# A fused Mamba and quantised-FFN kernel: copies out of PSUM one or two slots later in ScalarE's order, and z's first quarter in the other PSUM bank

## The chip, the core and the metric

The kernel runs on 1 core of one Trainium2 chip. The metric is the device time of one execution in microseconds (us); less is better. Engines go by the profile's names: PE is TensorE's matmuls and PEld its weight loads, DVE is VectorE, ACT is ScalarE, POOL is GpSimd, SP is SyncE.

## What is computed

Two inputs of 2 x 2048 tokens are folded into one stream, and one layer adds two branches to it. Cut to what matters here:

```python
# branch 1: a small conditioning scan, then a Mamba block (D_INNER 1024, D_STATE 16)
xn = layernorm(cond_scan(x))                       # 64 states, projection back to 512
x_br, z = split(xn @ W_in)                         # 1024 and 1024
xb = silu(causal_conv4(x_br) + conv_b)
Bm, Cm = xb @ W_b, xb @ W_c                        # 16 and 16
delta = softplus(xb @ W_delta + b_delta)           # 1024
h = exp(delta * A) * h + delta * Bm * xb           # per channel and state, over 2048 steps
y = sum(h * Cm) + xb * Dp
x = x + (y * silu(z)) @ W_out + residual
# branch 2: low-rank modulated layer, then a bit-linear FFN 512 -> 2048 -> 512 with GELU
x = x + ffn(cond2(x, cond))
```

## The kernel before

The file has two phases. `scan_phase` does branch 1, `ffn_phase` branch 2; the change is in `scan_phase` alone.

**Blocks and slots.** The 4096 tokens are cut into 16 blocks of 256 (`NBLK`, `T`). Every engine runs the same list of steps (`run_steps`): step -1 prepares block 0, step k scans block k while it prepares block k+1 and finishes block k-1, step 16 finishes the last block. A step has 32 slots (`NQ`), one for each of 8 channel tiles of 128 (`dt`) times 4 groups (`g`) of 4 states. All orders are written out by hand, slot by slot; engines meet only at semaphores, and each engine takes its own list strictly in order.

**What one slot q is.** ACT computes four `exp(delta * A)` into one of two PSUM buffers `a_ps` (L688, with `wait(act, s_scan, NQ * k + q - 1)`: the scan of slot q-2 has to be done). DVE multiplies u by B into one of four ring buffers (L842, helper `bx`), one slot ahead, and runs the scan (L850, helper `scans`). POOL saves the last column (L462) and multiplies the ring buffer by C in two halves (L469). PE sums the states by transposing each half into `yT_ps` (L1053, helper `turn_states`), and only then is the ring buffer free: `bx(q)` waits until `turn_states(q-4)` is done (`wait(dve, s_tr, NQ * k + q + 1 - RING)`). In slots 3 mod 4 `bx` first refreshes a column of B (L833, L839), and in slots 7, 15, 23 also computes u from delta and xb (L821); in slots 1 mod 4 DVE gates a finished tile with z (L785).

**The work beside the scan.** The other matmuls go to two PSUM banks, `work[0]` and `work[1]`. The table `BANK` names the bank of every job and, by its order, the turn: PE's `give(job)` waits until the job before it in the same bank has been copied out, and ACT's `take(job)` waits until PE has filled it. The jobs of block k+1 in the order of step k are: PRJ, WO0, WO1, YT, YB (conditioning scan and layer norm), XB0 to XB3 (x and the convolution, L992, copied by `xcopy`, L562), a Silu over x (`silu`, L571, with two ACT table loads around it), Z0 to Z3 (the quarters of z, L1000, copied by `zcopy`, L555; silu of z in `zsilu`, L579), BC (B and C, L1008, which needs the finished Silu, copied by `bc`, L585), and DL0 to DL3 (delta, L1019; `dexp`, `dtail`, `dln` are L597/L599, L606, L610, with a table load at L610 and one back at L688). Between them stand WOUT0 and WOUT1 (output rows of block k-1, L1035, copied by `wout`, L513) and GT0 to GT3 (gated tiles, L1063, copied by `gT`, L620). PE's slots are in the dictionary `plan`, ACT's in `next_plan`, `scan_plan`, `turned` and `back_plan`. y0 goes back through `y0back` (L533, L535), and x(0, 0) waits for it.

**Delta's second part** is one addition of 128x1024 elements on POOL (`delta_sum`, L420). `SUMS = (27, 6)` gives its slots: in 27 for the first half of the next block, in 6 for the second half of this block; in POOL's list it stands ahead of that slot's L462 and L469.

```python
def give(job):
    wait(pe, free[BANK[job]], jobs_before(job, k))
    return work[BANK[job]]
def take(job, step_of=k):
    act.wait_ge(full[BANK[job]], jobs_before(job, step_of) + 1)
    return work[BANK[job]]
```

Of the kernel before, what the change touches and what calls it, by code (L numbers as in the profile page):

```python
# [19 lines left out]
ND = DI // P  # L20
# [21 lines left out]
NV = 228  # L42


SUMS = (27, 6)
BANK = {"PRJ": 0, "GT3": 1, "WOUT0": 1, "WO0": 0, "WO1": 0, "WOUT1": 1, "YT": 0, "YB": 0, "GT0": 1,
        "XB0": 0, "XB1": 1, "XB2": 0, "XB3": 1, "Z0": 0, "BC": 0, "GT1": 1, "Z1": 1, "DL0": 0,
        "DL1": 1, "Z2": 0, "Z3": 0, "GT2": 1, "DL2": 0, "DL3": 1}
BACK = ["GT3", "WOUT0", "WOUT1"]
TURN = ["GT0", "GT1", "GT2"]  # L50
# [18 lines left out]
def wait(eng, sem, value):  # L69

    if isinstance(value, int) and value <= 0:
        return
    eng.wait_ge(sem, value)


def scan_phase(nc, V, big, s_big, vec, xT_in, w_p, w_s, w_o, w_in, w_bc, w_delta, w_out, f_w1, f_w2, c2_w1, c2_w2,
# [3 lines left out]
    with ctx:  # L80
# [271 lines left out]
        def _(pool):  # L352
# [61 lines left out]
            def delta_sum(pair, b, bp):  # L414

                for j in (2 * pair, 2 * pair + 1):
                    pool.wait_ge(free[BANK[f"DL{j}"]], jobs_before(f"DL{j}", b - 1) + 1)
                pool.wait_ge(s_dln, 2 * b + pair + 1)
                d = delta[:, bp, 4 * pair:4 * pair + 4, :].rearrange("p a b -> p (a b)")
                nc.gpsimd.tensor_tensor(d, d, ln_full[:, :], ALU.add).then_inc(s_delta, 1)  # L420

            def step(k, par, front, back, scan):
                for q in range(NQ):
                    dt, g = q // NG, q % NG
                    if scan and q == SUMS[1]:
                        delta_sum(1, k, par)
                    if front and q == SUMS[0]:
                        delta_sum(0, k + 1, 1 - par)
# [46 lines left out]
        def _(act):  # L475
# [8 lines left out]
            def step(k, par, front, back, scan):  # L484
                n, fp = k + 1, 1 - par
# [19 lines left out]
                def wout(tt):  # L505
                    job = f"WOUT{tt}"
                    ps = take(job)

                    if tt:
                        act.wait_ge(s_st[0], 16 * k)  # L510
                    else:
                        act.wait_ge(s_st[1], 16 * k)
                    nc.scalar.activation(x2row[:, :], ps[:, :], ACT.Copy).then_inc(free[BANK[job]], 1)  # L513

                def stats(tt):
                    job = f"WO{tt}"
# [33 lines left out]
                def zcopy(j):  # L550
                    ps = take(f"Z{j}")
                    if j == 0:

                        wait(act, s_gate, ND * k)
                    nc.scalar.activation(zs[:, fp, j // 2, 512 * (j % 2):512 * (j % 2) + 512], ps[:, :], ACT.Copy)\  # L555
                        .then_inc(free[BANK[f"Z{j}"]], 1)

                def xcopy(j):
                    ps = take(f"XB{j}")
                    for m in range(2):  # L560
                        mt = 2 * j + m
                        r = nc.scalar.activation(xb[:, fp, mt, :], ps[:, T * m:T * m + T], ACT.Identity,  # L562
                                                 bias=V[:, V_CB + mt:V_CB + mt + 1])
                    r.then_inc(free[BANK[f"XB{j}"]], 1)
# [22 lines left out]
                def dexp(j, late):  # L587

                    ps = take(f"DL{j}", k - 1 if late else k)
                    b = k if late else n  # L590
                    if j >= 2:

                        act.wait_ge(s_delta, 2 * b + 1)
                    for m in range(2):
                        mt = 2 * j + m
                        bias = V[:, V_BD + mt:V_BD + mt + 1]
                        nc.scalar.activation(lnbuf[:, j % 2, T * m:T * m + T], ps[:, T * m:T * m + T], ACT.Abs,  # L597
                                             bias=bias).then_inc(s_dexp, 1)
                        r = nc.scalar.activation(delta[:, par if late else fp, mt, :], ps[:, T * m:T * m + T],  # L599
                                                 ACT.Relu, bias=bias)  # L600
                    r.then_inc(free[BANK[f"DL{j}"]], 1)

                def dtail(pair, late):
                    b = k if late else n
                    act.wait_ge(s_dexp, 8 * b + 4 * pair + 4)
                    nc.scalar.activation(ln_full[:, :], ln_full[:, :], ACT.Exp, scale=-1.0).then_inc(s_dmin, 1)  # L606

                def dln(pair, late):
                    act.wait_ge(s_dmin, 2 * (k if late else n) + pair + 1)
                    nc.scalar.activation(ln_full[:, :], ln_full[:, :], ACT.Ln, bias=1.0).then_inc(s_dln, 1)  # L610
# [6 lines left out]
                def gT(pair, gp):  # L617

                    ps = take(f"GT{pair}")
                    nc.scalar.activation(xb[:, gp, 2 * pair:2 * pair + 2, :],  # L620
                                         ps[:, :].rearrange("p (m t) -> p m t", m=2), ACT.Copy)\
                        .then_inc(free[BANK[f"GT{pair}"]], 1)
# [8 lines left out]
                def rowcopy(c):  # L631
# [4 lines left out]
                    else:  # L636
# [2 lines left out]


                next_plan = {5: [prj], 6: [prj_ln], 8: [lambda: stats(0)], 9: [lambda: stats(1)], 10: [y0scale],
                             11: [y0back], 13: [lambda: xcopy(0)], 14: [lambda: xcopy(1)], 16: [lambda: xcopy(2)],
                             17: [lambda: xcopy(3), silu], 18: [lambda: zcopy(0)], 19: [bc], 21: [lambda: zcopy(1)],
                             23: [lambda: dexp(0, False)], 26: [lambda: zcopy(2)],
                             27: [lambda: dexp(1, False), lambda: dtail(0, False), lambda: zcopy(3)],
                             28: [lambda: dln(0, False)], 30: [zsilu], 31: [lambda: dexp(2, False)]}
                scan_plan = {2: [lambda: dexp(3, True), lambda: dtail(1, True)], 6: [lambda: dln(1, True)]}
                turned = {13: 0, 20: 1, 28: 2}
                back_plan = {6: [lambda: gT(ND // 2 - 1, fp)], 9: [lambda: wout(0)], 11: [lambda: wout(1)]}
                for q in range(NQ + 1):  # L650
                    dt, g = q // NG, q % NG
                    if scan and q == FIRST[1] + 3:
# [33 lines left out]
                    for i in range(G):  # L686
                        s = G * g + i
# [199 lines left out]
        def _(pe):  # L887
# [13 lines left out]
            def step(k, par, front, back, scan):  # L901
                n, fp = k + 1, 1 - par
# [121 lines left out]
                def wout(tt, part):  # L1024
                    job = f"WOUT{tt}"
                    ps = work[BANK[job]]
                    if part == 0:
                        give(job)

                        pe.wait_ge(free[BANK["GT3"]], jobs_before("GT3", k) + 1)  # L1030
                        pe.wait_ge(s_c0, 6 * k)
                        kept = y0[:, :] if isinstance(k, int) and k == NBLK else y0k[:, fp, :]
                        pe.matmul(ps[:, :], kept[:, P * tt:P * tt + P], Wo[:, :], start=True, stop=False)
                    for d in ((0, 1), (2, 3, 4), (5, 6, 7))[part]:
                        r = pe.matmul(ps[:, :], xb[:, fp, d, P * tt:P * tt + P], Wout[:, d, :],  # L1035
                                      start=False, stop=(d == ND - 1))
                    if part == 2:
                        r.then_inc(full[BANK[job]], 1)
# [48 lines left out]
                def factor_row(c):  # L1087
# [6 lines left out]
                    for d in range(KD):  # L1094
# [9 lines left out]
                        9: [("n", turn_back), ("b", wout, 1, 2)], 10: [("n", x, 0, 0)],  # L1104
                        11: [("s", turn_gated, 0, k), ("n", x, 0, 1)], 12: [("n", x, 1, 0), ("n", x, 1, 1)],
                        13: [("n", x, 2, 0)], 14: [("n", x, 2, 1), ("n", x, 3, 0)], 15: [("n", x, 3, 1)],
                        16: [("n", z, 0)], 17: [("n", bc)], 18: [("s", turn_gated, 1, k)],
                        19: [("n", z, 1), ("n", dl, 0, 0)], 20: [("n", dl, 0, 1)],
                        21: [("n", dl, 0, 2), ("n", dl, 0, 3)], 22: [("n", dl, 1, 0)],
                        23: [("n", dl, 1, 1), ("n", dl, 1, 2)], 24: [("n", dl, 1, 3), ("n", z, 2)], 25: [("n", z, 3)],  # L1110
                        26: [("s", turn_gated, 2, k), ("n", dl, 2, 0)], 27: [("n", dl, 2, 1)],
                        28: [("n", dl, 2, 2), ("n", dl, 2, 3)], 29: [("n", dl, 3, 0)],
                        30: [("n", dl, 3, 1), ("n", dl, 3, 2)], 31: [("n", dl, 3, 3)]}
                if isinstance(k, int) and k == 0:

# [542 lines left out]
```

## Time and profile before

| what | value |
|---|---|
| time, median of 3 runs | 2754.73 us (2754.4 to 2756.45) |
| the profiled execution: its time, its span | 2753.85 us, 2751.0 us |
| first scan starts (end of step -1) | 117.34 us |
| scans of blocks 0 to 14, start to start of the next block | 1963.03 us together |
| block 15 and step 16, then the FFN | the rest of the span |
| busy: PE, DVE, ACT, POOL | 2349.6, 2281.2, 1717.7, 1727.1 us |
| granted TensorE clock, mean | 0.937 |

The span is what the hardware profiler covers, and the time is 2.85 us more. Times in rows are microseconds from the span's start. A row of the timeline may hold several like instructions in a run (xN), with the time from the first start to the last end. The bracket is idle time of that engine before the row and what ended it; a semaphore wait of several conditions is put down to the one that came last. An fp32 matmul counts twice in xN, a transpose once.

### The profile page before, as it was taken

Reading aid. Unit: us, or ns where it says so; the run is one execution under the profiler, and the core shown is the slowest. Engines: PE = TensorE matmul, PEld = TensorE weight load, DVE = VectorE, ACT = ScalarE, POOL = GpSimd, SP = SyncE. Lnnn points to the kernel's source line nnn. Section 1 sums busy time; section 2 is a strip of 40 time slices with the busy share of each in tenths; the row PEclk is TensorE's granted clock in tenths of the full one; section 3 lists DMA queues with packets and bytes.
Section 4 is the critical chain, followed back from the end, with each engine's and each line's share of the span. In section 5 each row is a group of like instructions: output and inputs, shape, how many; then the busy total and the mean of one; then the engine's idle time right before and its main releaser. Section 6 shows DMA issues by size and latency. Waiting matters only on the chain. (4 is left out here: it accounts for less than half of the span.)

```text
span 2751.0 us, 34252 instructions
## 1 busy us (share of the span) xinstructions
PE 2349.6 (85%) x11520; PEld 1605.6 (58%) x11520; DVE 2281.2 (83%) x2232; ACT 1717.7 (62%) x3379; POOL 1727.1 (63%) x2042
## 2 busy tenths in 40 slices
PE   7888888888898988888888888888888675999997
PEld 5656666666666666657566666656666222444443
DVE  2399999999898989898999999999988645788886
ACT  2557675767667676767676757576766334555554
POOL 0277777777787777777777777777777530322321
PEclk8889999999999999999999999999998896999999
DMA  4102020202010110101020202020103631121110
GB/s 180 70 1 70 9 73 5 73 7 75 17 62 22 56 52 27 63 16 70 9 69 9 69 9 72 6 73 5 70 13 114 241 117 57 54 69 57 57 62 23
DMA packets 47434, 151.72 MB, mean 55 GB/s; under 512 B 7973, under 2 KB 8869, under 8 KB 44206
## 3 DMA queue, kind: packets, MB, share of 16 engines
q1 hardware_dynamic: 47278, 149.76, 15.3%
q8 instruction: 83, 1.36, 0.2%
q14 instruction: 73, 0.60, 0.1%
HBM read 132.37 MB, written 17.37 MB: 54 GB/s over the span
## 5 line engine op out<-in xcount | busy, mean ns | idle before, releaser
L469 POOL TENSOR_TENSOR ring<-ring,Cbc 128x512 f32<-128x512 f32 x1024 | 1280.9, 1272 | 44.5 <-POOL carry L462 0.4
L850 DVE TENSOR_TENSOR_SCAN ring<-a_ps,ring 128x1024 f32<-128x1024 f32 x512 | 1168.0, 2281 | 139.7 <-ACT a_ps L688 138.7
L688 ACT ACTIVATE a_ps<-delta,nA 128x255 f32<-128x255 f32 x2048 | 847.8, 466 | 268.8 <-DVE ring L850 267.9
L1053 PE MATMUL yT_ps<-ident,ring 128*128 128x128 f32 x4096 | 590.2, 286 | 171.7 <-POOL ring L469 168.8
L842 DVE TENSOR_TENSOR ring<-u_ps,Bbc 128x1024 f32<-128x1024 f32 x512 | 618.7, 1208 | 28.1 <-PE yT_ps L1053 21.3
L1053 PEld LDWEIGHTS yT_ps<-ident,ring 128*128 128x128 f32 x4096 | 478.6, 145 | 278.7 <-POOL ring L469 239.3
L1019 PE MATMUL work<-xb,big 128*128 128x256 f32 x2048 | 488.4, 391 | 14.8 <-ACT zs L555 14.8
L1019 PEld LDWEIGHTS work<-xb,big 128*128 128x128 f32 x2048 | 393.9, 198 | 77.5 <-ACT zs L555 19.2
L462 POOL TENSOR_TENSOR carry<-ring,half 128x4 f32<-128x4 f32 x512 | 127.4, 249 | 434.8 <-DVE ring L850 432.0
L992 PE MATMUL work<-y0s,big 128*128 128x256 f32 x1024 | 235.1, 380 | 3.4 <-ACT y0s L535 2.6
L1035 PE MATMUL work<-Wout,xb 128*128 128x512 f32 x512 | 237.8, 599 | 0.0
L1393 POOL TENSOR_TENSOR m<-m,pows 128x1 f32<-128x1 f32 x64 | 34.1, 549 | 311.2 <-DVE m L1525 311.2
L992 PEld LDWEIGHTS work<-y0s,big 128*128 128x128 f32 x1024 | 188.1, 190 | 30.0 <-ACT y0s L535 5.6
L1035 PEld LDWEIGHTS work<-Wout,xb 128*128 128x128 f32 x512 | 98.6, 198 | 117.3 <-issue 117.3
L420 POOL TENSOR_TENSOR delta<-delta,lnbuf 128x1024 f32<-128x1024 f32 x32 | 75.3, 2354 | 103.2 <-ACT lnbuf L610 103.2
L1008 PE MATMUL work<-xb,Wbc 128*32 128x256 f32 x256 | 90.2, 530 | 52.4 <-ACT zs L555 52.4
L562 ACT ACTIVATE xb<-work,V 128x256 f32<-128x256 f32 x128 | 53.8, 471 | 122.0 <-PE work L992 122.0
L1460 PE MATMUL o_ps<-q,qhT 128*128 128x512 bf16 x512 | 119.1, 387 | 11.9 <-DVE qhT L1558 11.9
L1424 PE MATMUL x_ps<-lay,x2T 128*128 128x512 f32 x256 | 121.8, 620 | 0.7 <-ACT x2T L1485 0.7
L1439 PE MATMUL h_ps<-q,qaT 128*128 128x512 bf16 x512 | 115.7, 379 | 0.0
L597 ACT ACTIVATE lnbuf<-work,V 128x256 f32<-128x256 f32 x128 | 60.1, 470 | 86.1 <-PE work L1019 86.1
L821 DVE TENSOR_TENSOR u_ps<-delta,xb 128x510 f32<-128x510 f32 x64 | 70.4, 1100 | 49.5 <-POOL delta L420 49.5
(199 smaller groups left out, 2599.3 us busy)
## 6 DMA issues: line engine op xcount, KB each, us to landing
Bbc<-bc_rows SPq DMA_DIRECT2D x64, 512.0 KB, 4.7
Cbc<-bc_rows SPq DMA_DIRECT2D x64, 512.0 KB, 3.7
xT<-in_xT SPq DMA_DIRECT2D x16, 514.0 KB, 3.5
x_rows<-x2row SPq DMA_DIRECT2D x32, 256.0 KB, 2.0
xp<-x_rows SPq DMA_DIRECT2D x32, 256.0 KB, 2.7
xx<-in_x SPq DMA_DIRECT2D x32, 256.0 KB, 2.9
out_rows<-orow SPq DMA_DIRECT2D x32, 256.0 KB, 2.0
delta<-in_c_w SPq DMA_DIRECT2D x6, 1024.0 KB, 5.0
```

Source lines behind the costliest of these rows:

```text
L462: nc.gpsimd.tensor_tensor(carry[:, par, dt, G * g:G * g + G].rearrange("p (g o) -> p g o", o=1), h[:, :, T - 1:T], ident1, ALU.mult).then_ ...
L469: nc.gpsimd.tensor_tensor(hp, hp, Cbc[:, G * g + GP * c:G * g + GP * c + GP, :], ALU.mult)\
L688: r = nc.scalar.activation(a_ps[q % 2][:, i, 1:T], delta[:, par, dt, 1:T], ACT.Exp, scale=nA[:, dt, s:s + 1])
L842: dve.tensor_tensor(ring[:, q % RING, :, :], u_ps[:, dt % 2:dt % 2 + 1, :].to_broadcast([P, G, T]), Bbc[:, G * g:G * g + G, :], ALU.mult). ...
L850: dve.tensor_tensor_scan(ring[:, q % RING, :, :].rearrange("p g t -> p (g t)"), a_ps[q % 2][:, :, :].rearrange("p g t -> p (g t)"), ring[: ...
L992: r = pe.matmul(ps[:, T * m:T * m + T], Mx[:, tap, c:c + P], y0s[:, fp, tap:tap + T], start=(tap == 0), stop=(tap == 3))
L1019: r = pe.matmul(ps[:, T * m:T * m + T], Wd[:, d, c:c + P], xb[:, fp, d, :], start=(d == 0), stop=(d == ND - 1))
L1035: r = pe.matmul(ps[:, :], xb[:, fp, d, P * tt:P * tt + P], Wout[:, d, :], start=False, stop=(d == ND - 1))
L1053: r = pe.matmul(yT_ps[:, tt, :], ring[:, q % RING, i, P * tt:P * tt + P], ident[:, :], is_transpose=True, start=False, stop=(g == NG - 1 a ...
L1424: r = pe.matmul(x3_ps[:, :], x2T[:, d, :], lay[:, batch, d, :], start=(d == 0), stop=(d == KD - 1))
L1439: r = pe.matmul(h_ps[:, 512 * c:512 * c + 512], qaT[:, d, :], q1[:, d, 512 * c:512 * c + 512], start=(d == 0), stop=(d == KD - 1))
L1460: r = pe.matmul(o_ps[:, :], qhT[:, d, :], q2[:, d, :], start=(d == 0), stop=(d == KF - 1))
```

## The change

It edits tables of slot numbers only. No instruction is added or removed. On ACT the copies of x's first two parts (L562), z's quarters (L555), B and C (L585), the second output row tile (L513) and delta's first part (L597, L599) stand one to three slots later. Z0 goes from bank 0, ahead of BC, to bank 1, behind GT1, and on PE its matmul goes from slot 16 to slot 19; Z1, parts of DL0, DL1, DL2, DL3 and Z3 follow up to one or two slots later. On POOL the two additions L420 go from slot 27 to 28 and from 6 to 5.

```diff
-SUMS = (27, 6)
+SUMS = (28, 5)
 BANK = {"PRJ": 0, "GT3": 1, "WOUT0": 1, "WO0": 0, "WO1": 0, "WOUT1": 1, "YT": 0, "YB": 0, "GT0": 1,
-        "XB0": 0, "XB1": 1, "XB2": 0, "XB3": 1, "Z0": 0, "BC": 0, "GT1": 1, "Z1": 1, "DL0": 0,
+        "XB0": 0, "XB1": 1, "XB2": 0, "XB3": 1, "BC": 0, "GT1": 1, "Z0": 1, "Z1": 1, "DL0": 0,
         "DL1": 1, "Z2": 0, "Z3": 0, "GT2": 1, "DL2": 0, "DL3": 1}
...
-                             11: [y0back], 13: [lambda: xcopy(0)], 14: [lambda: xcopy(1)], 16: [lambda: xcopy(2)],
-                             17: [lambda: xcopy(3), silu], 18: [lambda: zcopy(0)], 19: [bc], 21: [lambda: zcopy(1)],
-                             23: [lambda: dexp(0, False)], 26: [lambda: zcopy(2)],
-                             27: [lambda: dexp(1, False), lambda: dtail(0, False), lambda: zcopy(3)],
-                             28: [lambda: dln(0, False)], 30: [zsilu], 31: [lambda: dexp(2, False)]}
+                             11: [y0back], 14: [lambda: xcopy(0)], 15: [lambda: xcopy(1)], 16: [lambda: xcopy(2)],
+                             17: [lambda: xcopy(3), silu], 20: [bc], 21: [lambda: zcopy(0)], 23: [lambda: zcopy(1)],
+                             25: [lambda: dexp(0, False)], 27: [lambda: zcopy(2), lambda: dexp(1, False), lambda: dtail(0, False)],
+                             28: [lambda: zcopy(3), lambda: dln(0, False)], 30: [zsilu],
+                             31: [lambda: dexp(2, False)]}
                 scan_plan = {2: [lambda: dexp(3, True), lambda: dtail(1, True)], 6: [lambda: dln(1, True)]}
                 turned = {13: 0, 20: 1, 28: 2}
-                back_plan = {6: [lambda: gT(ND // 2 - 1, fp)], 9: [lambda: wout(0)], 11: [lambda: wout(1)]}
+                back_plan = {6: [lambda: gT(ND // 2 - 1, fp)], 9: [lambda: wout(0)], 12: [lambda: wout(1)]}
...
                         9: [("n", turn_back), ("b", wout, 1, 2)], 10: [("n", x, 0, 0)],
                         11: [("s", turn_gated, 0, k), ("n", x, 0, 1)], 12: [("n", x, 1, 0), ("n", x, 1, 1)],
                         13: [("n", x, 2, 0)], 14: [("n", x, 2, 1), ("n", x, 3, 0)], 15: [("n", x, 3, 1)],
-                        16: [("n", z, 0)], 17: [("n", bc)], 18: [("s", turn_gated, 1, k)],
-                        19: [("n", z, 1), ("n", dl, 0, 0)], 20: [("n", dl, 0, 1)],
-                        21: [("n", dl, 0, 2), ("n", dl, 0, 3)], 22: [("n", dl, 1, 0)],
-                        23: [("n", dl, 1, 1), ("n", dl, 1, 2)], 24: [("n", dl, 1, 3), ("n", z, 2)], 25: [("n", z, 3)],
-                        26: [("s", turn_gated, 2, k), ("n", dl, 2, 0)], 27: [("n", dl, 2, 1)],
-                        28: [("n", dl, 2, 2), ("n", dl, 2, 3)], 29: [("n", dl, 3, 0)],
+                        17: [("n", bc)], 18: [("s", turn_gated, 1, k)],
+                        19: [("n", z, 0), ("n", dl, 0, 0)], 20: [("n", dl, 0, 1)],
+                        21: [("n", z, 1), ("n", dl, 0, 2)], 22: [("n", dl, 0, 3), ("n", dl, 1, 0)],
+                        23: [("n", dl, 1, 1)], 24: [("n", dl, 1, 2), ("n", dl, 1, 3)], 25: [("n", z, 2)],
+                        26: [("s", turn_gated, 2, k), ("n", z, 3)], 27: [("n", dl, 2, 0)],
+                        28: [("n", dl, 2, 1), ("n", dl, 2, 2)], 29: [("n", dl, 2, 3), ("n", dl, 3, 0)],
                         30: [("n", dl, 3, 1), ("n", dl, 3, 2)], 31: [("n", dl, 3, 3)]}
```

What the tables make of the order is seen at three places of a middle block.

PE, slots 16 and 17 (L1053 is the transposing of states, L1000 z's quarter, L1008 B and C), before:

```order
L1053 MATMUL yT_ps<-ident,ring 128x128 [waits s_hc]
L1053 MATMUL yT_ps<-ident,ring 128x128 x3
L1000 MATMUL work<-big,y0s 128x512 [waits bank_free0]
L1008 MATMUL work<-xb,Wbc 32x256 [waits s_xb,bank_free0]
L1008 MATMUL work<-xb,Wbc 32x256 x7
L1047 MATMUL yT_ps<-ident,xdp 128x128 [waits s_xdp,s_gate]
```

and after the change:

```order
L1053 MATMUL yT_ps<-ident,ring 128x128 [waits s_hc]
L1053 MATMUL yT_ps<-ident,ring 128x128 x3
L1008 MATMUL work<-xb,Wbc 32x256 [waits s_xb,bank_free0]
L1008 MATMUL work<-xb,Wbc 32x256 x7
L1047 MATMUL yT_ps<-ident,xdp 128x128 [waits s_xdp,s_gate]
```

BC's `bank_free0` is the copy of Z0 before, and the copy of XB2 after.

ACT, slots 27 and 28 (L555 is a copy of a quarter of z, L597 to L610 are delta's parts, L620 is a gated tile, L688 the exponentials), before:

```order
L606 ACTIVATE lnbuf<-lnbuf 128x1024 [waits s_dexp]
L555 ACTIVATE zs<-work 128x512 [waits bank_full0]
L688 ACTIVATE a_ps<-delta,nA 128x255 [waits s_scan]
L688 ACTIVATE a_ps<-delta,nA 128x255 x3
L610 ACT_TABLE_LOAD
L610 ACTIVATE lnbuf<-lnbuf 128x1024 [waits s_dmin]
L620 ACTIVATE xb<-work 128x512 [waits bank_full1]
L688 ACT_TABLE_LOAD [waits s_scan]
```

and after the change:

```order
L606 ACTIVATE lnbuf<-lnbuf 128x1024 [waits s_dexp]
L688 ACTIVATE a_ps<-delta,nA 128x255 [waits s_scan]
L688 ACTIVATE a_ps<-delta,nA 128x255 x3
L555 ACTIVATE zs<-work 128x512 [waits bank_full0]
L610 ACT_TABLE_LOAD
L610 ACTIVATE lnbuf<-lnbuf 128x1024 [waits s_dmin]
L620 ACTIVATE xb<-work 128x512 [waits bank_full1]
L688 ACT_TABLE_LOAD [waits s_scan]
```

Z3's copy went behind the exponentials of slot 27. Z2's copy, which stood ahead of the exponentials of slot 26, is now the first row of slot 27, ahead of L597.

POOL, slots 5 to 7 (L420 is delta's addition, L462 and L469 are a slot's column and product with C, L380 and L383 belong to slot 7), before:

```order
L462 TENSOR_TENSOR carry<-ring,half 128x4 [waits s_scan]
L469 TENSOR_TENSOR ring<-ring,Cbc 128x512 [waits s_carry]
L469 TENSOR_TENSOR ring<-ring,Cbc 128x512
L420 TENSOR_TENSOR delta<-delta,lnbuf 128x1024 [waits s_dln,bank_free1,bank_free0]
L462 TENSOR_TENSOR carry<-ring,half 128x4 [waits s_scan]
L469 TENSOR_TENSOR ring<-ring,Cbc 128x512 [waits s_carry]
L469 TENSOR_TENSOR ring<-ring,Cbc 128x512
L380 TENSOR_TENSOR nrm<-nrm,half 128x2 [waits s_rstd,bank_free0,s_zero]
```

and after the change:

```order
L420 TENSOR_TENSOR delta<-delta,lnbuf 128x1024 [waits s_dln,bank_free1,bank_free0]
L462 TENSOR_TENSOR carry<-ring,half 128x4 [waits s_scan]
L469 TENSOR_TENSOR ring<-ring,Cbc 128x512 [waits s_carry]
L469 TENSOR_TENSOR ring<-ring,Cbc 128x512
L462 TENSOR_TENSOR carry<-ring,half 128x4 [waits s_scan]
L469 TENSOR_TENSOR ring<-ring,Cbc 128x512 [waits s_carry]
L469 TENSOR_TENSOR ring<-ring,Cbc 128x512
L380 TENSOR_TENSOR nrm<-nrm,half 128x2 [waits s_rstd,bank_free0,s_zero]
```

The addition now stands ahead of slot 5's product instead of slot 6's.

## Rows read from the trace of the kernel before

**Rows 1.** The page's list of costliest groups: lines L850 (scan) and L1008 (B, C).

```profile
L850 DVE TENSOR_TENSOR_SCAN ring<-a_ps,ring 128x1024 f32<-128x1024 f32 x512 | 1168.0, 2281 | 139.7 <-ACT a_ps L688 138.7
L1008 PE MATMUL work<-xb,Wbc 128*32 128x256 f32 x256 | 90.2, 530 | 52.4 <-ACT zs L555 52.4
```

**Rows 2.** Timeline, DVE: first scans of blocks 0, 4, 5, 15 (start, us, work).

```profile
117.34 2.29 DVE L850 TENSOR_TENSOR_SCAN ring<-a_ps,ring 128x1024 f32<-128x1024 f32 x1 [2.44 <-ACT a_ps L688]
...
640.67 2.28 DVE L850 TENSOR_TENSOR_SCAN ring<-a_ps,ring 128x1024 f32<-128x1024 f32 x1
...
771.05 2.28 DVE L850 TENSOR_TENSOR_SCAN ring<-a_ps,ring 128x1024 f32<-128x1024 f32 x1
...
2080.37 2.28 DVE L850 TENSOR_TENSOR_SCAN ring<-a_ps,ring 128x1024 f32<-128x1024 f32 x1
```

**Rows 3.** Timeline of block 4, slots 4 to 8, ACT, POOL, DVE, PE; last row slot 15.

```profile
657.78 1.04 ACT L610 ACTIVATE lnbuf<-lnbuf 128x1024 f32<-128x1024 f32 x1
...
664.13 0.20 POOL L462 TENSOR_TENSOR carry<-ring,half 128x4 f32<-128x4 f32 x1 [3.96 <-DVE ring L850]
...
666.87 2.35 POOL L420 TENSOR_TENSOR delta<-delta,lnbuf 128x1024 f32<-128x1024 f32 x1
667.28 2.50 DVE L821 TENSOR_TENSOR u_ps<-delta,xb 128x510 f32<-128x510 f32 x1
...
676.37 0.66 PE L1053 MATMUL yT_ps<-ident,ring 128*128 128x128 f32 x4 [0.57 <-POOL ring L469]
...
699.12 0.67 DVE L821 TENSOR_TENSOR u_ps<-delta,xb 128x510 f32<-128x510 f32 x1
```

**Rows 4.** Timeline of block 4, slots 10 to 14, ACT and PE.

```profile
682.43 0.60 ACT L513 ACTIVATE x2row<-work 128x512 f32<-128x512 f32 x1 [3.97 <-PE work L1035]
...
683.68 1.97 PE L992 MATMUL work<-y0s,big 128*128 128x256 f32 x8 [0.19 <-ACT y0s L535]
...
690.83 5.35 PE L992 MATMUL work<-y0s,big 128*128 128x256 f32 x24
```

**Rows 5.** Timeline of block 4, slots 16 to 19, ACT, DVE, PE.

```profile
703.37 0.84 ACT L562 ACTIVATE xb<-work,V 128x256 f32<-128x256 f32 x2 [1.94 <-PE work L992]
...
705.57 2.00 ACT L571 ACTIVATE xb<-xb 128x1024 f32<-128x1024 f32 x2
...
710.59 2.29 DVE L850 TENSOR_TENSOR_SCAN ring<-a_ps,ring 128x1024 f32<-128x1024 f32 x1 [2.37 <-ACT a_ps L688]
...
711.12 5.13 PE L1008 MATMUL work<-xb,Wbc 128*32 128x256 f32 x16 [3.23 <-ACT zs L555]
...
717.54 0.18 DVE L839 TENSOR_REDUCE Bbc<-big 128x16 f32<-128x16 f32 x1 [1.35 <-PE yT_ps L1053]
```

**Rows 6.** Block 5: the same matmul (timeline), and a stretch of it (windows, PEclk after POOL).

```profile
841.49 6.50 PE L1008 MATMUL work<-xb,Wbc 128*32 128x256 f32 x16 [3.24 <-ACT zs L555]
...
839.00:843.00 4.00, 1.51 (x4) 0.72 (x5) 2.05 (x1) 3.98 (x10) 0.98 (x1) 0.68 0.00 0
```

**Rows 7.** Timeline of block 4, slots 23 to 28, PE, ACT, DVE.

```profile
738.62 0.66 PE L1053 MATMUL yT_ps<-ident,ring 128*128 128x128 f32 x4 [0.24 <-POOL ring L469]
739.12 1.89 PE L1019 MATMUL work<-xb,big 128*128 128x256 f32 x8
740.85 1.02 PE L1000 MATMUL work<-big,y0s 128*128 128x512 f32 x2
...
741.90 0.60 ACT L555 ACTIVATE zs<-work 128x512 f32<-128x512 f32 x1 [4.50 <-PE work L1000]
742.40 1.66 ACT L688 ACTIVATE a_ps<-delta,nA 128x255 f32<-128x255 f32 x4
...
754.40 2.29 DVE L850 TENSOR_TENSOR_SCAN ring<-a_ps,ring 128x1024 f32<-128x1024 f32 x1 [2.43 <-ACT a_ps L688]
```

**Rows 8.** Timeline of step -1 (before the first scan), PE.

```profile
77.97 5.33 PE L1008 MATMUL work<-xb,Wbc 128*32 128x256 f32 x16 [3.93 <-ACT zs L555]
...
104.02 15.30 PE L1019 MATMUL work<-xb,big 128*128 128x256 f32 x56 [3.19 <-ACT zs L555]
```

## The prediction

> **What bounds the kernel now.** I read the list of costliest groups first. DVE's scans are 1168.0 us of work, and DVE stood idle for 139.7 us ahead of them, 138.7 of it waiting for ACT's exponentials; PE's matmul for B and C stood still for 52.4 us behind ACT's copies of z [rows 1]. So DVE is the engine on the path, and what can be won is its waits. The timeline gives the unit to count in: the scans of blocks 0 to 14 run from 117.34 to 2080.37, 1963.03 us or 130.87 a block, and block 4, the one I follow below, takes 771.05 - 640.67 = 130.38 [rows 2]. Whatever is won in a block is won 15 times. The FFN phase behind it is untouched, so nothing there changes sign or size.
>
> Reading block 4 slot by slot, three places matter.
>
> Slots 5 to 8: POOL idles 3.96 us for the scan of slot 5, although ACT's logarithm, all that delta's addition needs, is done at 657.78 + 1.04 = 658.82. After slot 5's product POOL starts the addition at 666.87, and DVE's next L821, which like it reads two SBUF tensors, starts at 667.28 and takes 2.50 us instead of 0.67 [rows 3]. It ends 0.56 us after the addition, so it was held up by it.
>
> Slots 16 to 19: ACT copies x's last part at 703.37, the Silu ends at 705.57 + 2.00 = 707.57, yet PE's matmul for B and C starts at 711.12, after 3.23 us of waiting for the copy of z's first quarter, which stands behind a table load and slot 17's exponentials. It runs 5.13 us, PE comes to slot 16's states late, the ring buffer comes free late, and DVE waits 1.35 us in slot 19 [rows 5]. In block 5 the same matmul takes 6.50 us, at a granted clock of 0.68 over the stretch around its start, after an equal wait [rows 6].
>
> Slots 26 to 28: ACT idles 4.50 us for z's third quarter and only then does slot 26's exponentials, delta's parts and so on; the scan of slot 28 waits 2.43 us [rows 7].
>
> **The change, part by part, per block.**
>
> *Delta's addition, slot 6 to 5.* It now fits in the 3.96 us of POOL's idle time: it can start when slot 4's product is done, 3.96 before 664.13, at 660.17 (the logarithm is done), and takes 2.35, so it ends at 662.5, before the scan of slot 5 does [rows 3]. L821 falls to 0.67: DVE is 2.50 - 0.67 = 1.83 us early in slot 7. Not all of it stays. PE at this place was kept by POOL for only 0.57 us [rows 3]; with that gone PE is the later one, and DVE meets it at the ring buffer in slots 9 and 11. y0back no longer stands behind the second output tile, for which ACT waited 3.97 us, so x(0, 0) loses its wait of 0.19 too and starts behind the states without a gap [rows 4]. That is 0.57 + 0.19 = 0.76 us by the waits, and I take 0.8, since PE then runs x without a pause from 690.83 on [rows 4] and x's last part sets when the Silu and slot 17's exponentials come. Its bounds are 0 (PE's whole list stays where it is) and 1.83 (all of it stays). It is nearest to PE's own rows, so 0.8.
>
> What x's later copies cost: nothing. xcopy(0) goes behind slot 13's exponentials, but PE needs it only for x(2, 0), which is the third of the three parts that start at 690.83 and take 5.35 [rows 4]; two thirds of that, 3.6 us, lie between. If this cover went, x would be late one for one in slot 17.
>
> *B and C ahead of z's first quarter.* The wait of 3.23 goes. The matmul starts at the end of the Silu, 707.57 - 0.8 = 706.8, ends at 711.9 even at its 5.13, and the states of slot 16 follow: before, 717.54 - 716.25 = 1.3 us lay between its end and DVE's release, so now the buffer is free at 713.2. DVE, arriving at 717.54 - 1.35 - 0.8 = 715.4, has 2.2 us to spare, and 0.8 with the 6.50 of block 5 [rows 5, 6]. So the wait goes in every block: 1.35 in block 4, and since the blocks average 130.87 against its 130.38, 1.84 on average [rows 2, 5].
>
> Here the rows show PE losing clock after it idled; under the Trainium skill's page "TensorE: Matmul & The Clock Gate", section "Why this matters for your kernels", idle gaps between bursts of matmuls are to be avoided because they throttle the clock. By that the shorter gap ahead of B and C could also spare the slow stretch; the sum doesn't count on it, as nothing waits for this matmul any more.
>
> *Slots 24 to 28.* Behind slot 23's states, which POOL releases at 738.62, stood one part of DL1 and Z2's matmul (2.23 us from 738.62 to 740.85). Now two parts of DL1 stand there, one part more: 740.85 - 739.12 = 1.73, say 1.8. ACT gets z's third quarter 1.8 later after that point, but slot 26's exponentials, 1.66, are done in the idle 4.50 ahead of it instead of behind it. The copy of Z3 moves within ACT's run from one side of slot 27's exponentials to the other, which is nothing for slot 28. All else between the copy at 741.90 and the scan at 754.40 stands as before. Slot 28 comes 1.8 - 1.6 = 0.2 later against DVE's own progress: +0.2 [rows 7]. Bounds: -1.6 (PE is not what z waits for) and +1.8 (the exponentials gain nothing). The nearest row is the 4.50 of idle time, larger than 1.66, so +0.2. POOL's other addition, 27 to 28, lets slot 27's product go 2.4 us earlier and has DVE's long wait of slot 28 to itself; 0.
>
> *Step -1.* B and C start 0.5 us earlier (the copy and its signal fall out of 3.93), z's first quarter, 1.02, is no longer hidden: +0.5, carried by PE to the end of the step [rows 7, 8]. Block 15 gains its own 0.8 from the addition or less. Together 0.
>
> *The clock.* PE gets new idle time, about 2 us ahead of slot 19's states, since it no longer lags. I allow one slow stretch in seven blocks, at the 6.50 - 5.13 = 1.37 that it cost before [rows 5, 6]: +0.2 a block.
>
> Sum: 15 x (-0.8 - 1.84 + 0.2 + 0.2) = -33.6 us. The profiled execution took 2753.85, which gives 2720.3; the median of the runs is 0.88 higher, 2754.73, and gives **2721**. A measurement of this kernel can tell about 0.2%, 5.5 us, from no change.
>
> **The rivals.**
>
> *A, the addition wins nothing.* PE's list is full (its x work runs without a gap), so slot 17 stays where it is; only slot 19 is won: 15 x (-1.84 + 0.2 + 0.2) = -21.6, 2733. For it: ACT's silu waits for PE, 1.94 us [rows 5]. Against it: PE's own waits of 0.57 and 0.19.
>
> *A page as a rule for the same place.* The L821 of 2.50 us is seen beside an addition that reads SBUF [rows 3]. The Trainium skill's "SBUF — State Buffer", section "Who interferes with whom", calls the pair of ports that VectorE shares with GpSimd an exclusive lock. By it the addition could collide in its new slot 5 just as well; that would be up to 1.8 us lost ahead of slot 6 for 1.83 won, rival A again. The rows speak against it: from 660.2 to 662.5 DVE runs no L821.
>
> *B, one slow stretch in every block on the path.* PE's clock falls for DL1 and Z2 or for x: -33.6 + 15 x (1.37 - 0.2) = -16, 2739.
>
> *C, no change.* Some copy that went back holds PE, and through the two banks x or delta comes 2.2 us late; 2754. It speaks against it that the covers found are 3.6 and 2.2 us.
>
> *D, slower: the whole run from slot 23's states to Z2 at the lower of the two clock levels.* PE reaches these states early, waits for POOL, and the idle time takes the clock from 2.4 to 1.2 GHz. Two parts of DL1 and Z2, 1.8 + 1.73 + 1.02 = 4.6 us, take 4.6 more, and z's third quarter goes to slots 27 and 28 one for one: 15 x (4.6 - 2.24) = +35, 2790. It decides from 2.24 us of lost PE time a block on; 2.6 is more than 0.2% slower. Against it: before, a PE wait of 0.24 stood there and no more [rows 7], and a slow stretch cost 1.37.
>
> **How the numbers follow.** My forecast has 0.70, A 0.12, B 0.08, C 0.05, D 0.05. All of the first three are faster by over 0.2%: 0.90; same 0.05; slower 0.05. The range starts where all of the 1.83 stays: 15 x (-1.83 - 1.84 + 0.2) = -52, 2703, so 2704; it takes in A and B and ends 5 us over B, at 2744.
>
> **What would show it.** In the changed profile: L821's mean falls from one long in four to 0.67 throughout; PE's B and C wait for the Silu, not for L555; DVE has no wait on L1053 in slot 19; a wait on L688 in slot 17 that is longer than 2.37, near 3.6, since DVE now arrives early there and PE's x is the limit; slot 28's wait near 2.9; a block of 128.4 to 128.6. A block over 129.5, or L821 still at 2.50, makes the prediction wrong; so does a DVE wait in slots 20 to 25, where I expect none.

## The result and the profile after

The changed kernel takes 2711.06 us (median of 4 runs, 2709.42 to 2711.82) against 2755.59 for the kernel before (4 runs): a ratio of 0.9838, 95% interval 0.9822 to 0.9854. That is 44.5 us less, where the prediction had 33.6 (its terms against 2753.85) and 2721. The profiled execution took 2711.78 with a span of 2709.7 and a mean granted clock of 0.951.

The list of groups, line L821 (u from delta and xb) of the kernel before:

```profile
L821 DVE TENSOR_TENSOR u_ps<-delta,xb 128x510 f32<-128x510 f32 x64 | 70.4, 1100 | 49.5 <-POOL delta L420 49.5
```

and lines L850, L1008 and L821 of the changed kernel:

```profile
L850 DVE TENSOR_TENSOR_SCAN ring<-a_ps,ring 128x1024 f32<-128x1024 f32 x512 | 1167.6, 2281 | 140.5 <-ACT a_ps L688 140.5
L1008 PE MATMUL work<-xb,Wbc 128*32 128x256 f32 x256 | 72.6, 448 | 33.2 <-ACT xb L571 33.2
L821 DVE TENSOR_TENSOR u_ps<-delta,xb 128x510 f32<-128x510 f32 x64 | 43.0, 672 | 51.2 <-POOL delta L420 51.2
```

The first row answers to [rows 1] and is a warning: DVE waits as long for ACT as before, 140.5 against 139.7 us, and the kernel is 1.6% faster. The waits ahead of scans moved from slot to slot; what went is time that DVE lost elsewhere: 27.4 us in L821 (43.0 us busy instead of 70.4) and 28.1 us of waits ahead of L839 in slot 19, of which about 10 come back in slots 9 and 11. B and C now wait for the Silu (L571) and no longer for the copies of z, and their matmul's mean fell from 530 to 448 ns.

Where it went is seen by the starts of scans. The timeline of the changed kernel, DVE, first scans of blocks 0, 4, 5 and 15, and of block 4 the scans of slots 7, 17 and 28, with L821 of slot 7 and L839 of slot 19:

```profile
121.00 2.29 DVE L850 TENSOR_TENSOR_SCAN ring<-a_ps,ring 128x1024 f32<-128x1024 f32 x1 [2.01 <-ACT a_ps L688]
...
631.91 2.28 DVE L850 TENSOR_TENSOR_SCAN ring<-a_ps,ring 128x1024 f32<-128x1024 f32 x1
...
658.51 0.67 DVE L821 TENSOR_TENSOR u_ps<-delta,xb 128x510 f32<-128x510 f32 x1
...
660.58 2.28 DVE L850 TENSOR_TENSOR_SCAN ring<-a_ps,ring 128x1024 f32<-128x1024 f32 x1
...
700.75 2.29 DVE L850 TENSOR_TENSOR_SCAN ring<-a_ps,ring 128x1024 f32<-128x1024 f32 x1 [3.59 <-ACT a_ps L688]
...
706.27 0.15 DVE L839 TENSOR_REDUCE Bbc<-big 128x16 f32<-128x16 f32 x1
...
743.28 2.29 DVE L850 TENSOR_TENSOR_SCAN ring<-a_ps,ring 128x1024 f32<-128x1024 f32 x1 [2.95 <-ACT a_ps L688]
...
759.93 2.28 DVE L850 TENSOR_TENSOR_SCAN ring<-a_ps,ring 128x1024 f32<-128x1024 f32 x1
...
2039.88 2.28 DVE L850 TENSOR_TENSOR_SCAN ring<-a_ps,ring 128x1024 f32<-128x1024 f32 x1
```

Against [rows 2, 5, 7]: blocks 0 to 14 take 2039.88 - 121.00 = 1918.88 us instead of 1963.03, which is 44.15 less and all of the gain. L839 in slot 19, which waited 1.35 us for PE, waits no more. Block 4 takes 128.02 instead of 130.38. Up to slot 17's scan it is 68.84 instead of 69.92 (-1.08); from there to slot 28's, 42.53 instead of 43.81 (-1.28); from there to the next block, 16.65 both times. Outside the blocks step -1 ends 3.66 us later in this execution, and what follows block 15's first scan is 0.8 shorter (669.8 against 670.6).

### The profile page after: what moved, and what is told of

Read it like the earlier page. It is cut to its first block and busy times, and to the rows that moved or that the text cites. A ratio compares the mean times of both kernels' runs of the same rounds, so it can differ in the third digit from the quotient of the medians.

```text
span 2709.7 us, 34252 instructions
## 1 busy us (share of the span) xinstructions
PE 2310.2 (85%) x11520; PEld 1583.5 (58%) x11520; DVE 2250.1 (83%) x2232; ACT 1730.3 (64%) x3379; POOL 1726.0 (64%) x2042
## 3 DMA queue, kind: packets, MB, share of 16 engines
q1 hardware_dynamic: 47278, 149.76, 15.7%
## 5 line engine op out<-in xcount | busy, mean ns | idle before, releaser
L469 POOL TENSOR_TENSOR ring<-ring,Cbc 128x512 f32<-128x512 f32 x1024 | 1281.1, 1272 | 44.6 <-POOL carry L462 0.4
L850 DVE TENSOR_TENSOR_SCAN ring<-a_ps,ring 128x1024 f32<-128x1024 f32 x512 | 1167.6, 2281 | 140.5 <-ACT a_ps L688 140.5
L688 ACT ACTIVATE a_ps<-delta,nA 128x255 f32<-128x255 f32 x2048 | 850.2, 464 | 369.8 <-DVE ring L850 368.6
L1053 PE MATMUL yT_ps<-ident,ring 128*128 128x128 f32 x4096 | 584.8, 282 | 203.5 <-POOL ring L469 201.4
L1053 PEld LDWEIGHTS yT_ps<-ident,ring 128*128 128x128 f32 x4096 | 470.1, 143 | 323.9 <-POOL ring L469 282.2
L1019 PE MATMUL work<-xb,big 128*128 128x256 f32 x2048 | 471.4, 381 | 12.6 <-ACT zs L555 12.6
L1019 PEld LDWEIGHTS work<-xb,big 128*128 128x128 f32 x2048 | 381.4, 191 | 77.9 <-ACT zs L555 17.0
L462 POOL TENSOR_TENSOR carry<-ring,half 128x4 f32<-128x4 f32 x512 | 125.1, 244 | 402.3 <-DVE ring L850 400.7
L1035 PE MATMUL work<-Wout,xb 128*128 128x512 f32 x512 | 242.3, 608 | 0.0
L1035 PEld LDWEIGHTS work<-Wout,xb 128*128 128x128 f32 x512 | 100.6, 201 | 120.7 <-issue 120.7
L420 POOL TENSOR_TENSOR delta<-delta,lnbuf 128x1024 f32<-128x1024 f32 x32 | 75.4, 2357 | 78.3 <-ACT lnbuf L610 78.3
L562 ACT ACTIVATE xb<-work,V 128x256 f32<-128x256 f32 x128 | 53.4, 468 | 103.8 <-PE work L992 103.8
L1491 ACT ACTIVATE hb<-hb 128x2048 f32<-128x2048 f32 x32 | 61.1, 1911 | 65.6 <-DVE hb L1544 65.6
L1008 PE MATMUL work<-xb,Wbc 128*32 128x256 f32 x256 | 72.6, 448 | 33.2 <-ACT xb L571 33.2
L1544 DVE SCALAR_TENSOR_TENSOR hb<-h_ps,m,b1r 128x2048 f32<-128x2048 f32 x32 | 75.2, 2350 | 27.8 <-PE h_ps L1439 27.8
```

What stands on the lines that cost most here:

```text
L462: nc.gpsimd.tensor_tensor(carry[:, par, dt, G * g:G * g + G].rearrange("p (g o) -> p g o", o=1), h[:, :, T - 1:T], ident1, ALU.mult).then_ ...
L469: nc.gpsimd.tensor_tensor(hp, hp, Cbc[:, G * g + GP * c:G * g + GP * c + GP, :], ALU.mult)\
L688: r = nc.scalar.activation(a_ps[q % 2][:, i, 1:T], delta[:, par, dt, 1:T], ACT.Exp, scale=nA[:, dt, s:s + 1])
L850: dve.tensor_tensor_scan(ring[:, q % RING, :, :].rearrange("p g t -> p (g t)"), a_ps[q % 2][:, :, :].rearrange("p g t -> p (g t)"), ring[: ...
L1019: r = pe.matmul(ps[:, T * m:T * m + T], Wd[:, d, c:c + P], xb[:, fp, d, :], start=(d == 0), stop=(d == ND - 1))
L1053: r = pe.matmul(yT_ps[:, tt, :], ring[:, q % RING, i, P * tt:P * tt + P], ident[:, :], is_transpose=True, start=False, stop=(g == NG - 1 a ...
```

## Experiments

Each set of runs was measured together with the kernel before, on the same chip; its medians over the three sets were 2755.57, 2754.57 and 2755.99. "A block" below is the mean of blocks 0 to 14 by the starts of their first scans, and stretches of slots are means over the same blocks, from the start of one scan to that of another, where no block is named.

### The two halves, alone

**e1_sum_alone**, on the kernel before:

```diff
-SUMS = (27, 6)
+SUMS = (27, 5)
```

> The kernel before with one number changed: delta's second addition on POOL in slot 5 instead of 6. Theory (the addition held up DVE's L821, and behind it PE's list takes part of the 1.83 us back): L821 at slot 7 takes 0.67 us, and a block gets 0.8 to 1.1 us shorter up to slot 17, 12 to 16 us in all: about 2741. Rival A (PE's list sets slot 17 by itself): L821 0.67 all the same, but slot 17's wait grows by the whole 1.83 and the time stays at 2755. Rival (all of it stays): 27 us, 2728.

Measured: 2731.88 us, ratio 0.9916 (0.9900 to 0.9933), so 23.7 less: outside my 12 to 16, between it and the rival that all stays. L821 is 0.70 us at the longest. A block has 129.53 us instead of 130.87, -1.34. Up to slot 17 it is 0.96 shorter, inside what I expected. The other 0.37 lies in slot 19: the kernel before had a wait of about 2.7 us there in every third block, and here it is 1.54 in nearly all. The trace ties this to the matmul for B and C: in the kernel before it took about 6.5 us in every third block (granted clock 0.55 over block 5's) and 5.07 to 5.33 in the others (0.68 over block 3's); in e1 only block 0 has the long form, 6.61, and the others take 5.16 to 5.33, but for one of 3.64. Its mean is 509 ns instead of 530. So shifting PE's list by a microsecond also changed where its clock falls, which I had not counted. The rest, 4 us, lies behind block 15's start; against it, step -1 ended 2.54 us later in this execution.

**e2_from_bc_on**, the changed kernel with its first half undone:

```diff
-SUMS = (28, 5)
+SUMS = (27, 6)
...
-... 14: [lambda: xcopy(0)], 15: [lambda: xcopy(1)], ...
+... 13: [lambda: xcopy(0)], 14: [lambda: xcopy(1)], ...
...
-... 12: [lambda: wout(1)]}
+... 11: [lambda: wout(1)]}
```

> The changed kernel with its first half undone: both additions in slots 27 and 6, x's first two copies in 13 and 14, the second output tile in 11. What stays is everything from B and C on: Z0 in bank 1 behind GT1 and the later copies of z, B, C and delta. Theory: DVE's wait in slot 19 goes in every block (about 1.9), slots 24 to 28 cost 0.16 more, so 15 x 1.75 = 26 us less than the kernel before, 2729; with the addition alone this makes up the whole gain, the parts add. Rival (the parts depend on each other: B and C come earlier only because x came earlier): under 15 us.

Measured: 2742.27 us, ratio 0.9954 (0.9938 to 0.9971): 13.3 less, half of what the theory had, and the rival's figure. The wait in slot 19 is gone, as the theory says, but a new one stands at the end of the block. Its timeline, DVE, slots 30 and 31:

```profile
761.97 2.29 DVE L850 TENSOR_TENSOR_SCAN ring<-a_ps,ring 128x1024 f32<-128x1024 f32 x1 [0.84 <-ACT a_ps L688]
765.83 2.29 DVE L850 TENSOR_TENSOR_SCAN ring<-a_ps,ring 128x1024 f32<-128x1024 f32 x1 [1.57 <-ACT a_ps L688]
```

Before and after the change slot 31 waits 0.89. The suspect was delta's first addition on POOL, back in slot 27 here, a move that the prediction costed at nothing.

### The addition in slot 27 or 28

**e7_sum0_back** is the changed kernel with `SUMS = (27, 5)`.

> The changed kernel with delta's first addition on POOL back in slot 27. Theory from the run that kept both additions back (its slot 31 waited 1.57 us instead of 0.89): the addition holds slot 27's product, PE's states and behind them DL2, which ACT waits for in slot 31: +0.6 to +0.7 us a block, +9 to +11 us, 2720 to 2722. Rival (the forecast's own: it costs nothing): 2711.

Measured: 2737.79 us, ratio 0.9940 (0.9924 to 0.9957), 26.7 more than the changed kernel. The mechanism is the one expected and its price is over twice the size. First its timeline, PE in slots 27 to 29 and ACT's first delta part of slot 31 (block 4):

```profile
747.25 0.66 PE L1053 MATMUL yT_ps<-ident,ring 128*128 128x128 f32 x4 [3.52 <-POOL ring L469]
...
749.39 8.28 PE L1019 MATMUL work<-xb,big 128*128 128x256 f32 x32
...
755.98 0.47 ACT L597 ACTIVATE lnbuf<-work,V 128x256 f32<-128x256 f32 x1 [1.26 <-PE work L1019]
```

and the changed kernel's at the same places:

```profile
740.90 0.66 PE L1053 MATMUL yT_ps<-ident,ring 128*128 128x128 f32 x4 [0.57 <-POOL ring L469]
...
742.62 7.07 PE L1019 MATMUL work<-xb,big 128*128 128x256 f32 x32
...
751.23 0.45 ACT L597 ACTIVATE lnbuf<-work,V 128x256 f32<-128x256 f32 x1
```

With the addition ahead of slot 27's product PE waits 3.52 us for POOL; the 32 rows of delta's matmuls behind it then take 8.28 us instead of 7.07, and ACT, which had no wait in slot 31, has one of 1.26. DVE waits 2.27 instead of 0.89 there, in all but the first two blocks (1.95 and 2.19). A block is 129.58, +1.65.

Why the price is twice the one expected is seen beside e2, from which I had taken it. Its timeline, PE, at the same place of block 4:

```profile
754.65 2.34 PE L1053 MATMUL yT_ps<-ident,ring 128*128 128x128 f32 x8 [3.51 <-POOL ring L469]
756.78 7.58 PE L1019 MATMUL work<-xb,big 128*128 128x256 f32 x32
```

PE waits as long, 3.51 us, but the 32 rows take 7.58 us; the granted clock over them is 0.93, where it is 0.85 over the 8.28 us of e7 and 1.00 over the 7.07 of the changed kernel. The 0.70 us between them is what slot 31 waits more in e7 than in e2 (2.27 against 1.57). The last 0.30 of the 1.65 lies ahead of slot 17: in slot 9 DVE waits 0.74 instead of 0.44 in block 4.

**e11_sum0_alone** is the kernel before with `SUMS = (28, 6)`.

> The kernel before with delta's first addition in slot 28 instead of 27 and nothing else. Theory (in the old order PE has DL2 early enough either way, slot 31 waits 0.89 us in both): 0 to -2 us, 2753 to 2756. Rival (slot 27's product is on the path in the old order too): -8 us or more.

Measured: 2755.19 us, ratio 0.9998 (0.9988 to 1.0007): no change, as expected. Slot 31 waits 0.89. So the same move is worth nothing in the old order and 26.7 us in the new one. In the new order three parts of DL2 stand behind slot 27's states instead of two. That this is what makes the difference is read from the order and was not tested by itself.

**e10_bc_on_28** is e2_from_bc_on with `SUMS = (28, 6)`.

> The run with only the half from B and C on, and with it delta's first addition in slot 28. Theory (that run lost 0.7 us a block in slot 31 to the addition in slot 27): slot 31 waits 0.89 us again, 15 x (-1.94 + 0.17) = 27 us less than the kernel before, 2726 to 2730. Rival (the parts depend on each other): no better than 2742.

Measured: 2731.93 us, ratio 0.9918 (0.9902 to 0.9935): 24.1 less than before, 2 short of the range given, and 10.3 less than e2. Slot 31 waits 0.89 again. A block has 129.16, -1.70, and 15 x 1.70 = 25.6. So B and C do not need the earlier x: slot 19's wait goes without it, and in e2 its gain was only hidden by the addition left in slot 27. The halves nearly add, -1.34 (e1) and -1.70 against -2.94 for the whole: 0.37 of e1's gain is in slot 19, where e10 has it too, and the earlier y0back, about 0.2 (e5), is in neither.

### Taking single moves back out of the changed kernel

**e3_sum_back**: `SUMS = (28, 6)`.

> The changed kernel with delta's second addition back in slot 6. Theory: L821 at slot 7 takes 2.5 us again and 0.8 to 1.1 us a block is lost ahead of slot 17: +12 to +17 us against the changed kernel, 2723 to 2728. Rival A (PE's list sets slot 17): +2 at most, with slot 17's wait 1.8 shorter than 3.60.

Measured: 2726.8 us, ratio 0.9901 (0.9885 to 0.9918), 15.7 more than the changed kernel. The timeline at slot 6, POOL and DVE, is [rows 3] over again:

```profile
661.46 2.35 POOL L420 TENSOR_TENSOR delta<-delta,lnbuf 128x1024 f32<-128x1024 f32 x1
661.87 2.50 DVE L821 TENSOR_TENSOR u_ps<-delta,xb 128x510 f32<-128x510 f32 x1
```

Slot 17's wait is 3.60, unchanged, so rival A, in which it would have taken up the 1.83, falls: moving one POOL instruction moves the whole chain, PE's x included (its first matmul starts 42.65 us into block 4 instead of 41.84).

**e4_x_back**: x's first two copies in slots 13 and 14.

> The changed kernel with x's first two copies back in slots 13 and 14. Theory: DVE waits about 1 us for exponentials in slot 14 again, as in the kernel before, and slot 17's wait is shorter by just that, since PE's x sets slot 17: 0 to +2 us, 2711 to 2713. Rival (a wait in slot 14 is lost time, and moving these copies is what brought the unforecast 0.3 us a block): +5 to +17 us.

Measured: 2710.12 us, ratio 0.9841 (0.9824 to 0.9857), 0.9 less than the changed kernel: nothing. DVE waits 1.14 us in slot 14 and 2.37 in slot 17, against 0 and 3.60 in the changed kernel. A wait ahead of a wait is free. Of the moves that give the change its name, this one does nothing.

**e5_wout_back**: the second output tile in slot 11.

> The changed kernel with the copy of the second output tile back in ACT's slot 11, ahead of y0back. Theory (it holds y0back and so PE's x(0, 0), but POOL's product of slot 11 catches most of it): 0.1 to 0.3 us a block, +2 to +5 us, 2713 to 2716. Rival (a whole wait for the tile, above 1 us a block): +15 us or more.

Measured: 2713.32 us, ratio 0.9852 (0.9836 to 0.9869), +2.3, and a block has 128.15, +0.22.

**e6_z2_ahead**: the copy of Z2 in slot 26.

```diff
-... 27: [lambda: zcopy(2), lambda: dexp(1, False), lambda: dtail(0, False)],
+... 26: [lambda: zcopy(2)], 27: [lambda: dexp(1, False), lambda: dtail(0, False)],
```

> The changed kernel with the copy of z's third quarter back ahead of slot 26's exponentials. Theory (those 1.66 us of exponentials now fill ACT's wait for Z2; ahead of them the copy puts them on the path): slots 26 to 31 come 1.5 to 1.7 us later in each block, +22 to +25 us, 2733 to 2736. Rival (ACT catches up before the block's end): under +8 us.

Measured: 2738.1 us, ratio 0.9939 (0.9922 to 0.9955), +27.0, slightly above the range. A block has 129.62, +1.69, almost the 1.66 of the four exponentials. Its timeline, DVE, slots 26 and 27:

```profile
740.94 2.29 DVE L850 TENSOR_TENSOR_SCAN ring<-a_ps,ring 128x1024 f32<-128x1024 f32 x1 [2.04 <-ACT a_ps L688]
744.93 2.29 DVE L850 TENSOR_TENSOR_SCAN ring<-a_ps,ring 128x1024 f32<-128x1024 f32 x1 [0.37 <-ACT a_ps L688]
```

The changed kernel has no wait in slot 26 and 0.91 in slot 27.

### One step further

The longest wait left is slot 17's 3.60 us, behind the Silu, while ACT itself waits 1.94 us just before for x.

**e8_silu_later**, on the changed kernel:

```diff
-17: [lambda: xcopy(3), silu], 20: [bc], ...
+18: [lambda: xcopy(3), silu], 20: [bc], ...
```

> The changed kernel with x's last copy and the Silu one slot later, behind slot 17's exponentials. Theory (slot 17's wait of 3.60 us is only the order of ACT's list; the exponentials fit in the 1.94 us in which ACT waits for x): slot 17's wait goes, slot 18 waits about 1 us, 2.6 us a block are won there, and PE gives back 0 to 1.6 of it before Z2: -15 to -39 us, 2672 to 2696. Rival (PE's list from B and C to Z2 is full and the wait only moves to slots 19 to 28): 2708 to 2713. Rival (B and C 0.6 us later and DVE earlier: slot 19 waits for PE again by more than is won): slower than 2713.

Measured: 2690.51 us, ratio 0.9762 (0.9745 to 0.9778). Timeline, DVE, slots 17 to 20 of block 4:

```profile
688.75 2.28 DVE L850 TENSOR_TENSOR_SCAN ring<-a_ps,ring 128x1024 f32<-128x1024 f32 x1
...
692.91 2.29 DVE L850 TENSOR_TENSOR_SCAN ring<-a_ps,ring 128x1024 f32<-128x1024 f32 x1 [0.77 <-ACT a_ps L688]
696.63 0.18 DVE L839 TENSOR_REDUCE Bbc<-big 128x16 f32<-128x16 f32 x1 [1.42 <-PE yT_ps L1053]
```

That is 20.6 less than the changed kernel, inside the range of the theory. Slot 17 waits no more and slot 18 waits 0.77, but slot 19's old wait for PE is back with 1.42, as the last rival had it: B and C hold slot 16's states again. In the two blocks in which the matmul for B and C took 6.44 us, slot 19 waited about 2.6.

**e9_bc_later** puts them behind these states:

```diff
-17: [("n", bc)], 18: [("s", turn_gated, 1, k)],
+18: [("n", bc), ("s", turn_gated, 1, k)],
```

> The run with the Silu behind slot 17's exponentials, and B and C on PE in slot 18 instead of 17, behind slot 16's states. Theory (the 1.1 to 1.5 us that DVE waits in slot 19 there is slot 16's states standing behind B and C): that wait goes, 15 x 1.4 = 21 us less, about 2670, if slots 20 to 31 stay as they are. Rival (B and C come later, and through the banks DL0, DL1 and Z2 come later): 2685 to 2695, with more waits in slots 26 to 28.

Measured: 2670.72 us, ratio 0.9694 (0.9678 to 0.9710), 40.3 less than the changed kernel and 85.3 less than the one before. Timeline, DVE, slots 18 to 20:

```profile
689.48 2.29 DVE L850 TENSOR_TENSOR_SCAN ring<-a_ps,ring 128x1024 f32<-128x1024 f32 x1 [0.77 <-ACT a_ps L688]
691.69 0.16 DVE L839 TENSOR_REDUCE Bbc<-big 128x16 f32<-128x16 f32 x1
...
695.54 1.23 DVE L842 TENSOR_TENSOR ring<-u_ps,Bbc 128x1024 f32<-128x1024 f32 x1 [0.24 <-PE yT_ps L1053]
```

The forecast of about 2670 was right. The 1.42 is gone, 0.24 stands a slot later, and slots 27 to 31 wait as in the changed kernel (0.92, 2.94, 0.84, 0.89). A block has 125.15. This is the fastest version of the study.

## Why the prediction was right, and where its sizes were off

**The addition, -0.8.** Right in mechanism: L821 falls to 0.67, and PE takes part of the 1.83 back, in slots 9 and 11, where DVE waits 0.44 and 0.28 us in block 4. The term was too small. Slots 5 to 17 are 1.14 us shorter on average (47.67 against 48.80); the addition is worth 0.96 of it alone (e1) and 1.09 taken back out (e3), and the earlier y0back 0.22 (e5). I had assembled the term from PE's two waits, 0.57 and 0.19, and both brackets say too little. PE's first L1035 behind the wait of 0.57 starts 676.86 - 640.67 = 36.19 us into block 4 before and 672.12 - 636.83 = 35.29 in e1, 0.90 earlier: without the wait all four groups of states run as one row of 1.91 us, with it they take 1.58 and 0.66. In the same way x(0, 0) started 1.23 us after the start of the states ahead of it and starts 0.88 after it now, 0.35 less for a bracket of 0.19. "x's later copies cost: nothing" is what e4 shows.

**Slot 19, -1.84.** Right: the wait is gone in every block. Slot 18 to slot 19 takes 3.53 us instead of 5.51, -1.98. The matmul starts with the Silu's end, as forecast:

```profile
697.89 3.61 PE L1008 MATMUL work<-xb,Wbc 128*32 128x256 f32 x16 [1.92 <-ACT xb L571]
```

**Slots 24 to 28, +0.2.** Measured: slots 23 to 28 take 21.14 instead of 20.97 us, +0.17, and slot 28 waits 2.95 where 2.9 was forecast. e6 shows the offset in it by itself: the exponentials in ACT's wait are worth 1.69 a block. The timeline of the changed kernel shows them there, ACT, slots 26 and 27:

```profile
727.77 1.67 ACT L688 ACTIVATE a_ps<-delta,nA 128x255 f32<-128x255 f32 x4 [1.64 <-DVE ring L850]
732.34 0.60 ACT L555 ACTIVATE zs<-work 128x512 f32<-128x512 f32 x1 [2.90 <-PE work L1000]
```

**The addition from 27 to 28, 0.** As a step from the kernel before this was right (e11). But that it is itself a cover was not named: without it the new order loses 1.65 us a block (e7). The forecast took it as a harmless companion; it is a condition of the gain.

**The clock, +0.2 a block.** Measured as nothing: slots 18 to 19 take 3.53 us in every block and slots 19 to 23 take 14.53 before and after. But PE still slows down. The matmul for B and C takes 3.61 us in 8 of blocks 0 to 14 and 5.30 in the other 7, in turn; block 5 is one of these. Its timeline, and the windows over the matmul of blocks 4 and 5 (PEclk after POOL):

```profile
825.81 5.30 PE L1008 MATMUL work<-xb,Wbc 128*32 128x256 f32 x16 [1.92 <-ACT xb L571]
...
697.89:701.50 3.61, 3.61 (x17) 1.71 (x18) 0.74 (x1) 3.60 (x8) 0.68 (x1) 1.00 0.00 0
825.81:831.11 5.30, 5.30 (x17) 2.25 (x18) 2.43 (x2) 4.52 (x10) 0.74 (x2) 0.68 0.02 3
```

So the granted clock is 1.00 over the one and 0.68 over the other, behind an equal wait of 1.92 us. The Trainium skill's page "TensorE: Matmul & The Clock Gate", section "Why this matters for your kernels", has gaps between bursts of matmuls as what costs the clock. The trace agrees in part: with the wait down from 3.23 to 1.92 us the form of 6.5 us is gone from the blocks, and 8 of the 15 run B and C at 2.4 GHz, which none did before. It also shows that the wait just ahead of a matmul doesn't settle its clock. The slow form costs nothing here because the states that DVE waits for are done in time with either; what sets which block is slow stays open.

**Step -1 and block 15, 0 together.** Step -1 ended 3.66 us later in the profiled execution. Two rows of PE show the parts, first of the kernel before, then of the changed one:

```profile
59.12 14.06 PE L992 MATMUL work<-y0s,big 128*128 128x256 f32 x64 [0.73 <-issue]
```

```profile
61.52 14.06 PE L992 MATMUL work<-y0s,big 128*128 128x256 f32 x64 [0.73 <-issue]
...
79.97 6.56 PE L1008 MATMUL work<-xb,Wbc 128*32 128x256 f32 x16 [4.39 <-ACT xb L571]
```

2.40 us are there ahead of any moved instruction: the start differs from one execution to the next (the first scan is at 117.34 in the kernel before and at 119.88 in e1, which has the same step -1). Of the remaining 1.26, counted from this row on, B and C start 0.40 earlier (0.5 was forecast) and take 1.23 longer, 6.56 against 5.33, and 0.43 come behind them, which fits the +0.5 for z's first quarter. The 1.23 is not the change's: in e1 and e11, with the old order in step -1, the same matmul took 6.26 and 6.19.

By block: 15 x (-1.14 - 1.98 + 0.17) = -44.2 us, the 44.15 measured in blocks. The forecast's 33.6 was short by 15 x 0.34 for the first term, 15 x 0.14 for the second, 15 x 0.03 for the third and 15 x 0.2 for the clock, 10.7 us together. For the same reason a block is 127.93 and not 128.4 to 128.6, the one sign of the list that did not come; the others did: L821 at 0.67, B and C waiting for the Silu, slot 17 at 3.60, slot 28 at 2.95, no wait in slots 20 to 25.

Of the rivals, A falls by e3. L821 beside the addition takes 2.50 us again in e3, but in slot 5 no instruction of DVE is held up: those beside the addition take as long as they did without it. B, a slow stretch on the path in every block, falls by the 3.53 and 14.53 us above. C's and D's waits do not appear. D's mechanism, PE waiting for POOL and then running at a lower clock, does show in e7, at another place and with 0.85 and not half. The move of z's first quarter to the other bank was never run apart from the rest of the second half, so how the 1.70 us of e10 divide among its moves is known only for slot 26 (e6).

## What to carry to other kernels

Count a step's gain where DVE actually starts its instructions, slot by slot, and not by the sum of its waits, which was 139.7 and 140.5 us here with 44 us between the kernels. In a list that an engine takes in order, work that is ready belongs in front of work that has to wait for another engine: exponentials ahead of the copy of Z2 gave 27 us, ahead of the Silu with B and C behind the states 40. A move that measures as nothing by itself can still be the cover of another one, so it is tested both alone on the old kernel and taken out of the new.

## What the runs showed of the hardware that I had not expected

A VectorE tensor_tensor that reads two SBUF tensors, issued 0.41 us after a GpSimd addition of 2.35 us, takes 2.50 us instead of 0.67, in each of the kernels that keep the addition in slot 6; this was expected from [rows 3]. Not expected was how far the granted clock of TensorE spreads a small shift: moving one GpSimd instruction (e1) changed how often the matmul for B and C took 6.5 us, its mean going from 530 to 509 ns, and made a wait of 2.7 us in every third block one of 1.54. Nor was it expected that an equal wait of 1.92 us ahead of this matmul is followed by 3.61 us (clock 1.00) and 5.30 us (0.68) in turn in the changed kernel, and by 3.61 in all blocks of e6 and e7. In e7 a PE wait of 3.52 us was followed by 32 rows of matmuls at 8.28 instead of 7.07 us (0.85), in e2 one of 3.51 by the same rows at 7.58 (0.93). And the same start of a program varied by 2.5 us between profiled executions.
